# Two orders of issue changed: attention passes taken in turns by head, weight preparation placed behind the sigmoid

## What is computed

```python
def attn(h):                       # h = layernorm(x)
    q = rmsnorm(rope(h @ wq_comp @ wq_up)) # 16 heads of 128
    k = rmsnorm(rope(h @ wk)); v = h @ wv  # one key/value head
    s = where(0 <= i - j < 512, q @ k.T / sqrt(128), -1e30)
    p = softmax(concat([s, sink]))         # per head, sliding window 512
    a = p[..., :t] @ v
    return (a.reshape(b, t, 4, 512) einsum out_w1) @ out_w2
def ffn(h):                        # h = layernorm(x)
    return (sigmoid(h @ Q(w1).T) * (h @ Q(w2).T)) @ Q(w3).T
def Q(w): return clip(round(w / (mean(abs(w)) + 1e-8)), -1, 1)
x = x + attn(layernorm(x)); x = x + ffn(layernorm(x))
```

## Time and profile before

| | us |
|---|---|
| two runs of the kernel, median | 8701.71 (8590.23 and 8813.19) |
| profiled execution | 8641.62 |
| its span on the slowest core, core 7 | 8640.1 |
| spans of all cores | 8542.3 to 8640.1 |
| PE busy with matmuls | 4674.5 (54%) |
| DVE busy | 2209.2 (26%) |
| ACT busy | 2098.6 (24%) |
| POOL busy | 104.3 (1%) |

### The profile page before, as it was taken

How to read it: one execution, slowest core, us unless ns; L and a number is a source line. 1 busy time by engine, 2 the same in 40 slices (tenths; PEclk the granted TensorE clock), 3 DMA queues, 4 the chain that set the end, 5 groups by cost and what they waited for, 6 DMA issues and landing times.

```text
span 8640.1 us, 62712 instructions; the slowest of 8 cores (8542.3 to 8640.1 us)
## 1 busy us (share of the span) xinstructions
PE 4674.5 (54%) x21684; PEld 2096.8 (24%) x21684; DVE 2209.2 (26%) x3806; ACT 2098.6 (24%) x2440; POOL 104.3 (1%) x149
## 2 busy tenths in 40 slices
PE   0002446677877355555454335765888355545555
PEld 0002213333333122222222212332333122222222
DVE  4533252320112122222123344221111222212222
ACT  0002111111002433333432211111100433343332
POOL 0000000000000000000000000000000000000000
PEclk9999655556887677777777565555899677777778
DMA  7642100004341545545654100001433344454444
GB/s 235 233 172 79 19 2 3 2 2 88 59 68 25 125 110 111 111 111 112 132 112 117 43 12 3 2 3 50 68 59 59 86 112 110 113 132 110 111 110 119
DMA packets 926022, 718.71 MB, mean 83 GB/s; under 512 B 596960, under 2 KB 850928, under 8 KB 903184
## 3 DMA queue, kind: packets, MB, share of 16 engines
q1 hardware_dynamic: 278224, 477.44, 18.8%
q10 hardware_dynamic: 558080, 138.55, 9.5%
q0 software_dynamic: 89408, 98.71, 7.3%
HBM read 657.89 MB, written 16.78 MB: 78 GB/s over the span
## 4 chain that ended last, share of the span: by engine, by line
PE 41%; ACT 18%; DVE 15%; DMA 10%; ACTq 8%; issue 7%; DVEq 1%; POOL 0%; SPq 0%; POOLq 0%
PE P L928 11%; PE P L1164 7%; ACT arena L1009 6%; ACT arena L1013 6%; PE P L1134 6%; DMA arena<-ffn_w 5%; ACTq L1040 5%; DVE arena L1016 4%; PE P L742 3%; PE P L737 3%; PE P L889 3%; DMA arena<-out_w 3%; ACTq L1074 2%; DVE red L682 2%; PE P L758 2%
## 5 line engine op out<-in xcount | busy, mean ns | idle before, releaser
L1134 PE MATMUL P<-arena 128*128 128x512 bf16 x2816 | 795.6, 446 | 1654.4 <-DVE arena L1145 1653.7
L1009 ACT ACTIVATE arena<-arena,b_m,invg 128x1024 bf16<-128x1024 f32 x528 | 653.8, 1238 | 1981.7 <-issue 1678.7
L928 PE MATMUL P<-arena 128*128 128x512 bf16 x4096 | 933.7, 394 | 6.9 <-ACT arena L902 6.9
L1016 DVE TENSOR_TENSOR arena<-arena 128x1024 bf16<-128x1024 bf16 x528 | 364.6, 691 | 1858.9 <-ACT arena L1013 1858.9
L1134 PEld LDWEIGHTS P<-arena 128*128 128x128 bf16 x2816 | 306.5, 111 | 2129.4 <-issue 1910.3
L1013 ACT ACTIVATE arena<-arena,b_p,invg 128x1024 bf16<-128x1024 f32 x528 | 654.6, 1240 | 49.9 <-ACT arena L1009 0.8
L1112 PE MATMUL P<-arena 128*128 128x512 bf16 x2816 | 627.0, 381 | 29.9 <-DMA arena<-arena 29.9
L1164 PE MATMUL P<-arena 128*128 128x512 bf16 x2816 | 614.9, 379 | 8.2 <-DVE arena L1179 6.8
L928 PEld LDWEIGHTS P<-arena 128*128 128x128 bf16 x4096 | 411.5, 101 | 529.2 <-issue 169.3
L341 PE MATMUL PT<-idn,arena 128*128 128x128 bf16 x1152 | 145.8, 307 | 696.9 <-DVE arena L653 270.7
L939 DVE TENSOR_TENSOR arena<-arena,P 128x512 f32<-128x512 f32 x256 | 176.2, 688 | 1297.5 <-PE P L928 1297.5
(11 more groups left out here) (116 smaller groups left out, 3460.3 us busy)
## 6 DMA issues: line engine op xcount, KB each, us to landing
arena<-ffn_w SPq DMA_DIRECT2D x528, 512.0 KB, 4.2
arena<-ffn_w SPq DMA_DIRECT2D x120, 1024.0 KB, 6.0
arena<-out_w POOLq DMA_DIRECT2D x64, 1024.0 KB, 12.3
arena<-h SPq DMA_DIRECT2D x40, 1024.0 KB, 5.6
arena<-out_w POOLq DMA_DIRECT2D x8, 2048.0 KB, 24.9
out<-arena SPq DMA_DIRECT2D x16, 1024.0 KB, 4.4
arena<-ffn_w SPq DMA_DIRECT2D x16, 768.0 KB, 4.3
arena<-arena ACTq DMA_TRANSPOSE x528, 5.1
```

The costliest lines, as they stand in the source:

```text
L928: e.matmul(P.P0[:, (j % 4) * 512: (j % 4) * 512 + 512], P.bf(O_Y1 + kc2 * 1024 + j * 128, 128), P.bf(O_W2QS[s3] + (kc2 % 8) * 512, 512), s ...
L1009: t1 = P.op("scalar", lambda e: e.activation(out=P.bf(O_S1, 1024), in_=P.f32(src_off, 1024), func=AF.Sign, bias=P.b_m05[:], scale=P.invg[: ...
L1016: t3 = P.op("vector", lambda e, dst=dst: e.tensor_tensor(out=dst, in0=P.bf(O_S1, 1024), in1=P.bf(O_S2, 1024), op=ALU.add), waits=[t2])
L1134: e.matmul(P.P1[:, 1024:1536], P.bf(d2 + kc * 128, 128), P.bf(O_LN2T + kc * 1024 + nn * 512, 512), start=(kc == 0), stop=(kc == NKC - 1)),
```

## The change

Two orders of issue change; no instruction is added or removed. In `ph_d` the two passes are cut into functions for one head, and head hh of pass 1 of tile j is followed by head hh of pass 2 of tile j-1; the transposes at the end of a pass are a function of their own. In `ph_g` the call prep(c + 1) moves from ahead of chunk c's first matmuls to behind its sigmoid, and stays ahead of the matmuls by w2 and the products. The bodies of the attention functions are as before but for names, and are left out here.

```diff
-        def pass1(j):
...
-            for hh in range(H):
...
+        def pass1_head(j, hh):
...
-        def pass2(j):
+        def pass2_head(j, hh):
...
+            st["p2sc"][j] = t_sc
+            st["p2no"][j] = t_no
+
+        def pass2_tail(j):
+            msl = j % 2
+            t_no = st["p2no"][j]
+            t_sc = st["p2sc"][j]
             for hb in range(2):
...
-            pass1(j)
+            for hh in range(H):
+                pass1_head(j, hh)
+                if j > 0:
+                    pass2_head(j - 1, hh)
             if j > 0:
-                pass2(j - 1)
+                pass2_tail(j - 1)
             crow(j)
-        pass2(NT - 1)
+        for hh in range(H):
+            pass2_head(NT - 1, hh)
+        pass2_tail(NT - 1)
...
                 c = win * SG + cw
-                if c + 1 < NW:
-                    prep(c + 1)
                 d1, tk1, d2, tk2, w3d[cw], tk3 = preps.pop(c)
...
                     func=AF.Sigmoid, scale=0.5),
                     waits=[t_x1, hid_rd[cw], self.T_LN2, x2ps_rd])
                 x1ps_rd = t_sg
+                if c + 1 < NW:
+                    prep(c + 1)
                 t_hd = None
                 for nn in range(2):
```

More of the change, by code:

```diff
@@ L666, in ph_d @@
               "att_ev": None, "t_last": None, "t_sc": {}, "t_cm": {},
-              "crow_tok": {}}
-        def pass1(j):
+              "crow_tok": {}, "p2sc": {}, "p2no": {}}
+        def pass1_head(j, hh):
             jp = j % 2
-            t_cm = None
-            for hh in range(H):
[L673 to L695, removed]
@@ new lines, in pass1_head @@
+            par = hh % 2
+            psA = P.P0[:, par * 1024: par * 1024 + 640]
+            P.op("tensor", lambda e, j=j, hh=hh, psA=psA: e.matmul(
+                psA[:, 0:512], P.bf(O_QTN + (j * H + hh) * 128, 128),
+                P.bf(O_KT + j * 128, 512), start=True, stop=True),
+                waits=[self.T_QTN, self.T_KT, psA_free[par]], inc=False)
+            t_s = P.op("tensor", lambda e, j=j, hh=hh, psA=psA: e.matmul(
+                psA[:, 512:640], P.bf(O_QTN + (j * H + hh) * 128, 128),
+                P.bf(O_KT + (j + 4) * 128, 128), start=True, stop=True))
@@ L721, in pass2 @@
             t_mk = st["t_mk"][j]
-            t_no = None
+            par = hh % 2
+            psB = P.P1[:, 0:640]
+            psAt = P.P1[:, 1024:1153]
+            psDen = P.P1[:, 1152:1153]
             t_sc = None
[L724 to L784, removed]
@@ new lines, in pass2_head @@
+            for c in range(NCH):
+                blk = psB[:, c * 128:(c + 1) * 128]
+                P.op("tensor", lambda e, j=j, hh=hh, c=c, blk=blk:
+                     e.matmul(blk, P.bf(O_KT + (j + c) * 128, 128),
+                              P.bf(O_QTN + (j * H + hh) * 128, 128),
+                              start=True, stop=False),
+                     waits=[t_cr, t_mk, st["psB_free"]] if c == 0 else [],
+                     inc=False)
+                P.op("tensor", lambda e, hh=hh, blk=blk: e.matmul(
+                    blk, P.ones_r[:],
+                    P.AR[0:1, O_CRW + hh * 128: O_CRW + (hh + 1) * 128],
+                    start=False, stop=False), inc=False)
+                t_sc = P.op("tensor", lambda e, c=c, msl=msl, blk=blk:
+                            e.matmul(blk, P.iden[:],
+                                     P.bf(O_MKS + msl * 640 + c * 128,
+                                          128),
+                                     start=False, stop=True),
+                            inc=(c == NCH - 1))
@@ new lines, in pass2_head @@
+            t_ex = P.op("scalar", lambda e, par=par, psB=psB:
+                        e.activation(out=P.bf(O_PRB + par * 640, 640),
+                                     in_=psB, func=AF.Exp),
+                        waits=[t_sc] + (list(self.prev["store"])
+                                        if (r == 1 and j == 0
+                                            and hh < 2) else []))
+            st["psB_free"] = t_ex
+            t_at = None
+            for c in range(NCH):
+                pch = P.bf(O_PRB + par * 640 + c * 128, 128)
+                t_at = P.op("tensor", lambda e, pch=pch, psAt=psAt, j=j,
+                            c=c: e.matmul(
+                                psAt[:, 0:129], pch,
+                                P.bf(O_VN + (j + c) * VST, 129),
+                                start=(c == 0), stop=(c == NCH - 1)),
+                            waits=[t_ex, self.T_V, self.t_vone,
+                                   st["psC_free"]]
+                            if c == 0 else [], inc=(c == NCH - 1))
@@ new lines, in pass2_head @@
+            t_es = P.op("scalar", lambda e, hh=hh, jp=jp: e.activation(
+                out=P.dstat[:, 0:1],
+                in_=P.cmaxf[:, jp * H + hh: jp * H + hh + 1],
+                func=AF.Exp, bias=P.sinkb[:, hh:hh + 1], scale=1.0),
+                waits=[self.t_sink, st["t_cm"][j], st["t_dn"]])
+            t_dn = P.op("vector", lambda e, psDen=psDen: e.tensor_tensor(
+                out=P.dstat[:, 1:2], in0=psDen, in1=P.dstat[:, 0:1],
+                op=ALU.add), waits=[t_at, t_es])
@@ L785, in pass2 @@
+            st["psC_free"] = t_no
+            st["p2sc"][j] = t_sc
[4 more added lines that the diff above has]
+            t_sc = st["p2sc"][j]
             for hb in range(2):
```

30 lines of the change are left out of this document (28 added, 2 removed).

## The result

| | before | after |
|---|---|---|
| median of the runs side by side, us | 8706.0 (8575.87 to 8813.19, 10 runs) | 9147.08 (9065.41 to 9354.94, 11 runs) |
| ratio, with its 95% interval | | 1.061 (1.056 to 1.066) |
| profiled execution, us | 8641.62 | 9190.57 |
| spans of all cores, us | 8542.3 to 8640.1 | 9043.3 to 9189.0 |

The account below looks back on a forecast made before the run. Bound: feed-forward's serial ACT-DVE chain of prep plus 16 matmuls, with L1112 hidden. Profiled 8641.6 + 604 (feed-forward) - 133 (attention) gave 9,110 us, 5% slower, ratio 1.05; range 8,900 to 9,270.

Parts of the forecast that it names:

- The mechanism: Feed-forward: the product still waits for prep's six adds on DVE, so matmuls L1112 move onto the path; 604 us more.
- The size of a chunk: Feed-forward, sigmoid to sigmoid: 41.81 us against 34.64, 7.17 more; with a down projection 83.25 against 75.94, 7.31 more.
- The lower bound: Feed-forward: 16 matmuls and L1112 start at the higher clock already, loss 436 us, total 8,945; cheaper feed-forward had 0.07.
- the dearer one: Feed-forward: both matmul groups longer at the lower clock, 2 us more a chunk, 772 us; 0.08 shared with attention without gain.
- ACT idle: Feed-forward: ACT idle for about 12 us ahead of each sigmoid, as a sign in the changed trace.
- Attention: Attention: passes in turns make a tile 87.2 us against 96.72, saving 9.5 over 14 tiles, 133 us.
- The wait for the small DMA: Attention: the max row's DMA is no longer covered, so scores start about 2.3 us after the tile's first matmul.
- The rival in which PE and DVE eat the gain: Attention: heads 0.6 us longer from mutual waits, no gain, 9,246 us; 0.08 shared with a dearer feed-forward.
- The rival in which PE's clock rises in attention: Attention: busier PE leaves the 0.50 clock, total 8,730 us if all rises, 8,920 if half; chance 0.14.

Follow-up runs that it names:

- e3: Changed kernel with prep(c+1) moved behind both products of chunk c, sigmoid still ahead of prep on ACT; 8690.77 us, ratio 0.993 to the kernel before.
- e4: Changed kernel with 16 of the 32 matmuls by w1 per chunk left out; median span on cores 0 to 3 8737.6 us against 9059.0.
- e5: Kernel before with 16 of the 32 matmuls by w1 per chunk left out; spans 8555.7 to 8572.7 us against a median of 8556.5.
- e1: Changed kernel with prep put back where it was, so only attention's new order remains; 8472.13 us, ratio 0.990 to the kernel before.
- e8: On e1, the first pass's two matmuls of a head moved between scores and values; 8450.82 us, ratio 0.970 to the kernel before.
- e2: Kernel before with only prep moved behind the sigmoid, attention untouched; 9203.17 us, ratio 1.071 to the kernel before.
- e6: Changed kernel with prep cut: half-tiles 1 and 2 behind the first product, 3 to 6 behind the second; 8191.12 us, ratio 0.943 to before.
- e7: On e6, ahead of a down projection the last four half-tiles are spread over its row tiles 1 to 4; 7974.2 us, ratio 0.912 to before.

## Why the prediction was right, point by point

**The mechanism.** The step that carried it was to follow the moved call into each list it appends to: behind the sigmoid on ACT, but still ahead of the product on DVE. The changed timeline shows it as named (product right behind the sixth add, PE idle for 25.98 us where 25 was written), e3 shows that DVE's list and not ACT's is what costs, and e4 with e5 that the time lost is the matmuls by w1.

**The size of a chunk.** Term by term, predicted from the earlier trace rows and measured in the chunk shown above (core 4):

| term | predicted | measured |
|---|---|---|
| sigmoid to first sign pass | 0.92 | 0.93 |
| first sign pass to sixth add | 26.84 | 26.92 |
| add to product, product to matmuls | 0.61, 0.83 | 0.61, 0.83 |
| 16 matmuls by w2 | 5.54 | 6.07 |
| matmuls by w1 to the sigmoid | 7.07 | 7.22 |
| sum | 41.81 | 42.58 |

Two small misses: the last term was taken to the end of the matmul group in the earlier trace rows, the sigmoid starts 0.15 us after it; and the 16 matmuls, behind a longer stop of PE, run somewhat slower (mean of the line 454 ns for 446 in the earlier trace rows; 6.07 us is this chunk, and the mean of these 16 over all chunks of core 1, from their starts, is 5.6 for 5.4). On core 1 the plain interval is 42.0, or 7.4 over before for the predicted 7.17, and the one with a down projection 7.1 over for 7.31. The stage cost 616 us for 604. The lower bound (436, by a higher clock at once) and the dearer one (772) were both far off; the rows of before were the right price.

**ACT idle.** I wrote about 12 us before each sigmoid and it is 14.83. The 2.2 us between half-tiles that the earlier trace rows shows as a stop inside each of them end with the last one, so they belong to the wait; no time hangs on it.

**Attention.** Predicted 87.2 us a tile and 133 us in all; measured 88.59 (core 4) and 121 (core 1). The pair takes 0.53 us and not 0.49, 0.6 us over the 15 heads, and the wait before the values grew by 0.02 us a head (276.6 for 270.9 in all), 0.4 us a tile; the wait for the DMA adds 0.1, and 0.3 of the 1.4 us stay unexplained. The wait for the small DMA came as forecast: scores 2.39 us behind the tile's first matmul for 2.3. The rival in which PE and DVE eat the gain falls by the stage times of e1.

**The clock.** The rival in which PE's clock rises in attention had 0.14. The changed stage stayed at 0.50, and so did e8, whose waits before the values are 0.61 us a head. The stage is entered at that level: on core 1 of the changed kernel 1.00 was last granted until 1157 us, the attention's first matmul starts at 1176, and 1.00 comes back at 1953, with the output projections. No gap of PE within the stage is longer than 2.5 us. The Trainium skill (TensorE: Matmul & The Clock Gate, section "Why this matters for your kernels") names short idle gaps between bursts as the way to avoid drops of the rate. The prediction read it as a rule by which the stage would run at 2.4 GHz, which asks more of it, since the rate had dropped before the stage began. These traces show that with gaps of at most 2.5 us it wasn't raised; whether such gaps would have kept a full clock no run here shows.

**The sum and the range.** The profiled execution of after took 9190.57 us, 80 over the forecast, and its slowest core isn't explained by the two edits: on core 4 the output projections took 820.4 / 789.7 us, on core 0 747.8 / 742.8, which is 120 us more in a stage that the change doesn't touch (below). Core 0 ended at 9057.6. The kernel before had the same on core 7 in round 1 (810.7 for 744.5 on core 0), so I had a part of it in my base without seeing it. On core 1, which had it in neither kernel, the forecast's terms give 8565 + 604 - 133 = 9,036, and 9043.3 was measured. Taken as ratios, 1.054 was forecast and 1.061 measured.

## What to carry to other kernels

When a call that appends to several engines' lists is moved, write down for each engine what it now stands behind and what stands behind it; here the move freed the sigmoid on ACT and left the product, which needs the sigmoid, behind the same six adds on DVE. The cure isn't to move the whole helper but to cut it and drop its pieces into the waits of the engine that is the bottleneck of the chain: with the attention's new order in all of them, the same instructions gave 1.061 (whole, ahead of the products), 0.993 (whole, behind both), 0.943 (cut) and 0.912 (cut and spread). Insert work where the engine waits, not beside it: the same pair of matmuls ahead of the scores saved about 60 us a round, and between scores and values 117.

## What the hardware showed that I had not expected

In the output projections, where PE runs matmuls without a pause, two cores of a die were held at a clock between the two levels while the others had the full one. The same 50 us of the changed kernel, core 0, then core 4, then core 5 (span, busy and count of PE, weight loads, DVE, ACT, POOL; granted clock; DMA share; GB/s):

```profile
2200.00:2250.00 50.00, 49.79 (x229) 22.67 (x232) 9.64 (x14) 0.00 (x0) 3.52 (x4) 1.00 0.43 68
```

```profile
2200.00:2250.00 50.00, 50.00 (x192) 20.74 (x191) 8.26 (x12) 0.00 (x0) 3.51 (x4) 0.81 0.33 53
```

```profile
2200.00:2250.00 50.00, 50.00 (x192) 20.76 (x191) 8.26 (x12) 0.00 (x0) 3.52 (x4) 0.81 0.53 84
```

PE is busy throughout on all three, but cores 4 and 5 get 191 weight loads done where core 0 gets 232, in the proportion of the clocks (191 / 232 = 0.82). Over 2031 to 2650 us the mean granted clock is 0.82 on cores 4 and 5 and 0.88 to 0.91 on the other six. In the trace of before it is cores 6 and 7 that have 0.82 over the same stretch, and the other six 0.93. It costs core 4 some 45 to 75 us in a round's output projections (820.4 and 789.7 for 745). The feed-forward can have it too: from 3850 to 3890 us cores 6 and 7 of the changed kernel were at 0.81, and their feed-forward of that round took 2178.1 and 2170.9 us for 2140.5 on core 1. Nor is it always two cores: from 6450 to 6480 us all four of that die had 0.81. The Trainium skill (TensorE: Matmul & The Clock Gate, Part 1) describes a peak-current limiter of 13/16 of the full clock under dense matmuls of several cores, which would be 0.81; the size agrees with 0.81 here. That it takes a whole die agrees with those 30 us, but not with the 50 us above, in which cores 6 and 7 of the same die have 1.00. All eight cores run this stage, and in six of the eleven profiled executions (e1, e2, e3, e6, e7 and e8) no core was at 0.81 at any time. When it comes, and to which cores, stays open; no run was made on it.
